# Householder tridiagonalisation of a 512 x 512 graph matrix: a new order inside each column, and interleaved matmul units placed twice per column

## The chip, the cores and the metric

One core of a Trainium2 chip runs the whole program in one launch. The metric is the time on the device in microseconds; the median of 3 runs of the kernel before is 5769.74 us (5765.54 to 5769.83).

## What is computed

Inputs are features x (16 batches, 512 nodes, 128 features) and a 512 x 512 adjacency matrix. Two layers follow each other, all in float32.

The first layer is a graph diffusion by eight explicit Euler steps:

```python
h = jnp.einsum('bnd,ed->bne', x, fc_in_w) + fc_in_b
def euler_step(h, _):
    ax = jnp.einsum('nm,bmd->bnd', adj_mx, h)
    f = alph * 0.5 * (ax - h) + h @ w_eff - h + x0
    return (h + dt * f, None)
```

and then a layer norm of x + h. The second layer needs the eigenvectors of the normalised Laplacian of the same adjacency matrix:

```python
L_norm = d_inv_sqrt[:, None] * (jnp.diag(deg) - A) * d_inv_sqrt[None, :]
_, U = jnp.linalg.eigh(L_norm)
agg = jnp.einsum('mn,bnd->bmd', U.T, features)
out = jax.nn.relu(agg @ W1 + b1) @ W2 + b2
return jnp.einsum('nm,bmd->bnd', U, out)
```

followed by a residual and a second layer norm. The eigendecomposition needs nothing from the first layer, and the second layer's other products need it.

## The kernel before

**Phases.** The matrix is first reduced to tridiagonal form by 511 Householder columns, one after the other. Then come the layer norm, a QL iteration on 32 leaves, five merge levels and the back transformation, and the second layer's products. The change touches the first phase alone. It is 3.3 of the 5.8 milliseconds.

**One column.** The matrix lies as T = 4 row tiles of 128 partitions. Column k works on `n_on = 4 - (k+1)//128` tiles: four tiles for k up to 126, three for 127 to 254, two for 255 to 382 (these are the "wide" columns), one for 383 to 510 (the "narrow" ones). Updates of the matrix are kept as pending pairs (u, r), up to some twenty of them. Every 16 columns the pending pairs become a panel, and `panel_stage` adds it to the matrix over the next 3 + n_on columns. Each column has its extra panel matmul in the tensor block (L700 to L724) and its extra addition in `householder` (L1343).

The order is written out by hand, in one program per engine, with semaphores between them:

- VectorE, `householder` (L1317): `x_ready(k)` says that the column x is written (L1425 of the column before). Then `next_reflected(k-1)` (L1290) takes the pivot column from the matrix (L1286 to L1300), forms z (L1309), and multiplies it with u (L1311). Then it takes one product of matrix and x per tile (L1352), HK (L1357), the fixing of the pending pair (L1364, L1368), the norm RN (L1371), the corrections (L1286, L1288), Q and RB (L1378, L1379), y (L1386), RQ (L1391), the sums CY (L1394, L1395), INVB and NINVB (L1398, L1399), beta (L1401 or L1406), BETAQ (L1404), TMP (L1418) and at last the next column (L1425).
- TensorE: it spreads x over all partitions by one transpose per tile (L681), sums z times u over the partitions (L653, or L656 for a narrow column, in `reflected_product`), computes the dots of x with the pending pairs (L688, one matmul per tile), then does its share of Euler units and the panel matmul, and after that the sum of CY (L729 or L733) and the pivot row of the pending pairs (L673).
- ScalarE copies x into the u column (L1109, L1110) and writes a unit vector beside it (L1113), takes root and norms out of the dots (L1115, L1117), scales ucN, MB, yq and tcol (L1129 to L1138), finishes u (L1146), and stores the results of the Euler units.
- GpSimd computes the signs SG, GZ, GT, HAL and P0 (L948 to L953) and U1 (L956, L957). In its spare time, one piece per column, it prepares the terms of the Euler polynomial (`preparations`, L919).

A narrow column does much of the same on one tile, and its product of matrix and x runs on TensorE (L695).

**Euler units.** The first layer is written as a polynomial in the adjacency matrix, and it runs on TensorE between the column's own matmuls. The generator `euler()` (L521) yields after every small portion of one product, a "unit". There are 551 of them. `euler_units(k)` says how many units a column takes, and all of them come after the dots:

```python
return 2 if 84 <= k < P + 84 else 1 if 8 <= k < 3 * P - 1 else 0
```

Units that are not used up in the columns run after the last one, `for _ in state: pass` (L735). The ScalarE program takes the same number of units per column, at the end of its column, after L1146, and stores each finished product with `euler_stored`. A product waits until the bank that it writes is stored, and the first product of a stage waits until all before it are. The products that use the polynomial's terms wait for `terms_ready`.

Of the kernel before, what the change touches and what calls it, by code (L numbers as in the profile page):

```python
# [112 lines left out]
def eig_gnn(nc, x, adj, alpha, w, d, fcw, fcb, W1, b1, W2, b2, consts, out, stop=99):  # L113
    ctx = ExitStack()
    with ctx:
# [40 lines left out]
        sparks = sb("sparks", [P, P])  # L156
# [64 lines left out]
        e_ready = sem("e_ready")  # L221
# [163 lines left out]
        MB, SPART = small[:, 32:33], small[:, 33:34]  # L385
# [37 lines left out]
        def euler_units(k):  # L423

            return 2 if 84 <= k < P + 84 else 1 if 8 <= k < 3 * P - 1 else 0
# [68 lines left out]
        def _(pe):  # L494
# [26 lines left out]
            def euler():  # L521
# [82 lines left out]
                pe.wait_ge(terms_ready, 1)  # L604
                for grp in range(4):
                    cols = slice(grp * N, (grp + 1) * N)
                    for i in range(4):
# [9 lines left out]
                        for mat in (Mt, M2t):  # L617
# [8 lines left out]
                            yield  # L626
                    for third in (2, 1, 0):
# [20 lines left out]
            def reflected_product(k):  # L648

                tp, n_on, pp = window_of(k)  # L650
                pe.wait_ge(z_ready, k + 1)
                if n_on >= 2:
                    nc.tensor.matmul(ps[1][:, 0:1], ones[:, :], SPART, start=True, stop=True).then_inc(s_ready, 1)  # L653
                else:
                    pe.wait_ge(u_ready, k + 1)
# [4 lines left out]
            adds_done = 0  # L660
            for k in range(N - 1):
# [17 lines left out]
                if n_on > 1:  # L679
# [10 lines left out]
                last.then_inc(dots_ready, 1)  # L690
                if n_on == 1:
# [6 lines left out]
                for _ in range(euler_units(k)):  # L698
                    next(state, None)
# [205 lines left out]
        def _(pool):  # L905
            nc.gpsimd.memset(UR[:, :], 0.0).then_inc(pairs_zeroed, 1)
            z = Chain(pool, pool_chain)
            ts, tt = nc.gpsimd.tensor_scalar, nc.gpsimd.tensor_tensor
# [8 lines left out]
            ts(sparks[:, :], ident[:, 0:P], SPARK, None, ALU.mult).then_inc(constants_ready, 1)  # L917

            def preparations():  # L919
# [13 lines left out]
                for _ in range(32):  # L933
                    yield
# [65 lines left out]
        def _(act):  # L1000
# [101 lines left out]
            for k in range(N - 1):  # L1102
# [45 lines left out]
                for _ in range(euler_units(k)):  # L1148
                    next(state, None)
# [1054 lines left out]
```

## Time and profile before

| | us |
|---|---|
| median of 3 runs | 5769.74 |
| profiled execution, its own time | 5766.69 |
| its span | 5764.9 |
| mean granted TensorE clock | 0.584 |
| busy PE / DVE / ACT / POOL | 2979.9 / 4277.6 / 1168.7 / 772.8 |

The span is the time from the first to the last instruction of the profiled execution. Its own time is 1.8 us longer, and 3.1 us under the median of the runs. PE is TensorE, PEld its weight loads, DVE is VectorE, ACT is ScalarE, POOL is GpSimd. L1425 is line 1425 of the kernel. Busy shares are means over phases with different limits, so they are read stage by stage. A granted clock of 0.50 is TensorE at 1.2 GHz and 1.00 is 2.4 GHz. The records of the clock begin at 390 us, and a stretch without any record is printed as 1.00.

### The profile page before, as it was taken

To read this page: it belongs to the slowest core of one execution; us is meant where nothing else is said; L and a number is where in the kernel's file an instruction comes from. 1 tells how busy PE (TensorE), PEld (TensorE's weight loads), DVE (VectorE), ACT (ScalarE), POOL (GpSimd) and SP (SyncE) were. 2 spreads that over 40 slices of the span, in tenths; PEclk is the share of its full clock that TensorE was granted. 3 is DMA by queue.
4 is the path that set the end of the run, shared out by engine and by line. 5 is a ranking of instruction groups with operands and counts; after the bars stand their busy time and mean duration, and the time that the engine had idled before them with its cause. 6 is when DMAs were issued, how large, how long until landed. Compare 5 with 4: busy or idle time off the path is not lost.

```text
span 5764.9 us, 62262 instructions
## 1 busy us (share of the span) xinstructions
PE 2979.9 (52%) x10552; PEld 2130.6 (37%) x10553; DVE 4277.6 (74%) x24278; ACT 1168.7 (20%) x5396; POOL 772.8 (13%) x3659
## 2 busy tenths in 40 slices
PE   6888888888888887877666610000000001010277
PEld 5656666556556555455555510000000000000243
DVE  7888777666667666666676678888788898889624
ACT  2333333333333333333222200000000000000000
POOL 2122211111111121222112111111100000000000
PEclk9985556656655555555555555555555555555688
DMA  1000000000000000000000000000000000000000
GB/s 40 1 1 1 1 1 1 1 1 1 1 1 1 1 1 1 1 1 1 1 1 1 1 25 0 0 0 0 0 0 0 0 0 0 0 0 0 0 0 29
DMA packets 16075, 17.01 MB, mean 3 GB/s; under 512 B 3056, under 2 KB 12400, under 8 KB 15472
## 3 DMA queue, kind: packets, MB, share of 16 engines
q1 hardware_dynamic: 15216, 13.47, 0.7%
q14 instruction: 264, 2.16, 0.1%
q8 instruction: 83, 1.36, 0.1%
q10 hardware_dynamic: 512, 0.02, 0.0%
HBM read 9.25 MB, written 4.19 MB: 2 GB/s over the span
## 4 chain that ended last, share of the span: by engine, by line
DVE 51%; PE 28%; ACT 7%; issue 7%; POOL 5%; DVEq 1%; ACTq 0%; DMA 0%; POOLq 0%; another core or an unknown queue 0%
PE ps L688 9%; DVE h L2020 5%; PE ps L653 3%; PE ps L632 2%; PE ps L620 2%; DVE am L1286 2%; DVE c L1288 2%; DVE UR L1425 2%; DVE UR L1309 2%; DVE notafter L1300 2%; PE ps L640 1%; ACT c L1134 1%; PE ps L722 1%; POOL small L948 1%; DVE hT L1647 1%
## 5 line engine op out<-in xcount | busy, mean ns | idle before, releaser
L688 PE MATMUL ps<-UR 128*128 128x41 f32 (+17 forms) x2552 | 606.5, 382 | 0.6 <-issue 0.6
L688 PEld LDWEIGHTS ps<-UR 128*128 128x128 f32 x2552 | 569.9, 315 | 0.9 <-DVE UR L1425 0.8
L805 PE MATMUL ps<-ident,m 128*128 128x128 f32 x36 | 9.0, 428 | 822.6 <-DVE small L2120 822.6
L749 PE MATMUL ps<-ones,qs 32*1 32x1 f32 x16 | 1.5, 158 | 821.2 <-DVE qs L1755 821.2
L681 PE MATMUL ps<-ident,UR 128*128 128x128 f32 x1148 | 318.4, 409 | 188.3 <-DVE UR L1425 183.3
L948 POOL TENSOR_SCALAR small<-small 128x1 f32<-128x1 f32 x511 | 117.3, 229 | 2201.9 <-ACT small L1117 2184.4
L729 PEld LDWEIGHTS ps<-small,ones 128*128 128x128 f32 x766 | 190.3, 301 | 393.7 <-DVE am L1395 308.6
L1418 DVE SCALAR_TENSOR_TENSOR small<-small,ps 128x1 f32<-128x1 f32 x510 | 112.1, 220 | 295.8 <-PE ps L729 279.0
L673 PE MATMUL ps<-UR,ident 128*128 128x18 f32 (+2 forms) x1020 | 299.4, 381 | 46.7 <-DVE UR L1368 46.7
L1115 ACT ACTIVATE small<-ps 128x1 f32<-128x1 f32 x511 | 87.6, 171 | 1163.5 <-PE ps L688 1163.5
L805 PEld LDWEIGHTS ps<-ident,m 128*128 128x128 f32 x36 | 7.0, 223 | 824.6 <-DVE small L2120 824.6
L749 PEld LDWEIGHTS ps<-ones,qs 32*1 32x1 f32 x16 | 0.7, 75 | 822.1 <-issue 822.1
L2020 DVE RECIPROCAL h<-h 128x512 f32<-128x512 f32 (+2 forms) x50 | 295.6, 5913 | 1.7
L653 PE MATMUL ps<-small,ones 128*128 128x1 f32 x766 | 213.3, 348 | 149.1 <-DVE am L1311 144.6
L653 PEld LDWEIGHTS ps<-small,ones 128*128 128x128 f32 x766 | 180.8, 294 | 290.7 <-DVE am L1311 290.7
L673 PEld LDWEIGHTS ps<-UR,ident 128*128 128x128 f32 x1020 | 260.9, 314 | 57.7 <-DVE UR L1368 57.7
L1359 DVE RECIPROCAL small<-small 128x1 f32<-128x1 f32 x511 | 83.2, 163 | 265.0 <-ACT small L1115 262.3
L681 PEld LDWEIGHTS ps<-ident,UR 128*128 128x128 f32 x1148 | 176.4, 198 | 235.2 <-DVE UR L1425 229.9
L729 PE MATMUL ps<-small,ones 128*128 128x2 f32 x766 | 204.1, 336 | 98.1 <-DVE am L1395 91.0
L1129 ACT ACTIVATE c<-UR,small 128x4 f32<-128x4 f32 (+2 forms) x383 | 114.2, 298 | 688.0 <-DVE small L1398 688.0
L640 PE MATMUL ps<-G,hT 128*128 128x128 f32 x1024 | 241.1, 401 | 5.2 <-ACT hT L1084 5.2
L640 PEld LDWEIGHTS ps<-G,hT 128*128 128x128 f32 x1024 | 214.0, 299 | 30.4 <-issue 22.5
(687 smaller groups left out, 9130.0 us busy)
## 6 DMA issues: line engine op xcount, KB each, us to landing
out<-xs SPq DMA_DIRECT2D x4, 1024.0 KB, 4.5
m<-in_adj SPq DMA_DIRECT2D x1, 1024.0 KB, 5.2
before<-c_before SPq DMA_DIRECT2D x1, 1024.0 KB, 6.9
notafter<-c_notafter SPq DMA_DIRECT2D x1, 1024.0 KB, 8.1
sib<-c_sib SPq DMA_DIRECT2D x1, 448.0 KB, 9.7
eye<-c_eye SPq DMA_DIRECT2D x1, 256.0 KB, 2.7
iota<-c_iota SPq DMA_DIRECT2D x1, 256.0 KB, 3.0
leafsel<-c_leaf SPq DMA_DIRECT2D x1, 256.0 KB, 3.2
```

The source lines that it names most:

```text
L620: last = nc.tensor.matmul(ps[6 + n % 2][:, :], xs[:, j, b * D:(b + 1) * D], mat[:, j, :], start=(j == 0), stop=(j == T - 1))
L632: nc.tensor.matmul(ps[6 + n % 2][:, :], M3t[:, j, tile(m)], h[:, j, cols] if third else middle[:, j, :], start=(j == 0), stop=False)
L640: last = nc.tensor.matmul(ps[6 + n % 2][:, tile(i)], Zt[r][i][:, tile(m)], terms[STEP3 * third + r], start=(third == 2 and r == 0), stop=( ...
L653: nc.tensor.matmul(ps[1][:, 0:1], ones[:, :], SPART, start=True, stop=True).then_inc(s_ready, 1)
L673: nc.tensor.matmul(ps[4][:, 0:2 * npend], over(one), flat[:, tp, 2 * first:2 * k], start=True, stop=True).then_inc(pivot_row_ready, 1)
L681: last = nc.tensor.transpose(ps[0][:, j * P:(j + 1) * P], over(x_of(j)), ident[:, 0:P])
L688: last = nc.tensor.matmul(ps[2][:, 0:2 * npend + 3], over(x_of(j)), flat[:, j, 2 * first:2 * k + 3], start=(j == tp), stop=(j == T - 1))
L729: nc.tensor.matmul(ps[3][:, 8:10], ones[:, :], CY, start=True, stop=True).then_inc(cy_ready, 1)
L948: z.post(ts(SG, AL, 0.0, 0.5, ALU.is_ge, ALU.subtract))
L1286: h_(tt(mine.rearrange("p (t l s) -> p t l s", t=n_on, s=2), pairs[:, tiles, first:first + npend, :], swapped.unsqueeze(1).broadcast_to([P ...
L1288: return h_.mark(nc.vector.tensor_reduce(out[:, 0:n_on], mine.rearrange("p (t l) -> p t l", t=n_on), AX.X, ALU.add))
L2020: g(nc.vector.reciprocal(Rm, Rm))
```

## The change

It does five things. (1) `euler_units(k)` returns a pair: so many units between the spreading of x and the dots, and so many after the dots. Columns 8 and 9 take three after the dots, columns 10 to 254 one and one, columns 255 to 382 two after the dots. (2) In wide columns the sum of z times u (`reflected_product`) moves behind the dots, and the dots wait for the z and u columns of the column before (`zq_ready`, `u_ready`). (3) GpSimd forms HAL first, then P0, then GT, each with its own signal. (4) VectorE computes RB and INVB before y, and takes over ucN of wide columns and MB and tcol of narrow ones. A narrow column writes x and u with one instruction. (5) The unit vectors beside the pairs are written once at the start and no longer in every column, and the wait for the Euler terms moves behind the first products that don't need them.

```diff
-            return 2 if 84 <= k < P + 84 else 1 if 8 <= k < 3 * P - 1 else 0
+            return (0, 0) if k < 8 or k >= 3 * P - 1 else (0, 3) if k < 10 else (1, 1) if window_of(k)[1] > 2 else (0, 2)
...
                 pe.wait_ge(x_loaded, 16 * T)
-                pe.wait_ge(terms_ready, 1)
...
+                    if grp == 0:
+                        pe.wait_ge(terms_ready, 1)
                     for third in (2, 1, 0):
...
                     last.then_inc(row_ready, 1)
-                    if k:
-                        reflected_product(k - 1)
-                pe.wait_ge(xm_ready, k + 1)
-                pe.wait_ge(e_ready, k + 1)
+                for _ in range(euler_units(k)[0]):
+                    next(state, None)
+                if k <= narrow_from:
+                    pe.wait_ge(xm_ready, k + 1)
+                if k:
+                    pe.wait_ge(u_ready, k)
+                    pe.wait_ge(zq_ready, k)
                 for j in range(tp, T):
                     last = nc.tensor.matmul(ps[2][:, 0:2 * npend + 3], over(x_of(j)), flat[:, j, 2 * first:2 * k + 3],
                                             start=(j == tp), stop=(j == T - 1))
                 last.then_inc(dots_ready, 1)
+                if n_on > 1 and k:
+                    reflected_product(k - 1)
...
-                for _ in range(euler_units(k)):
+                for _ in range(euler_units(k)[1]):
                     next(state, None)
...
+            z.sync()
+            for t in range(T):
+                units = nc.gpsimd.tensor_copy(pairs[:, t, t * P:(t + 1) * P, 0], ident[:, 0:P])
+            units.then_inc(pairs_zeroed, 1)
...
-                for _ in range(32):
+                for _ in range(12):
                     yield
...
-                z.post(ts(SG, AL, 0.0, 0.5, ALU.is_ge, ALU.subtract))
-                z.post(ts(GZ, XN, 0.0, 0.5, ALU.is_le, ALU.subtract))
-                ts(GT, XN, 0.0, None, ALU.is_gt)
-                z.sync()
-                tt(HAL, AL, SG, ALU.mult)
+                z(ts(SG, AL, 0.0, 0.5, ALU.is_ge, ALU.subtract))
+                tt(HAL, AL, SG, ALU.mult).then_inc(signs_ready, 1)
+                z(ts(GZ, XN, 0.0, 0.5, ALU.is_le, ALU.subtract))
                 tt(P0, GZ, SG, ALU.mult).then_inc(signs_ready, 1)
+                ts(GT, XN, 0.0, None, ALU.is_gt).then_inc(signs_ready, 1)
...
-                if not final:
-                    nt, _, npp = window_of(k + 1)
-                    nc.scalar.activation(flat[:, nt, 2 * k + 4:2 * k + 5], ident[:, npp:npp + 1], ACT.Copy).then_inc(e_ready, 1)
...
-                    act.wait_ge(invb_ready, k + 1)
                     if n_on > 1:
-                        act.wait_ge(xm_ready, k + 1)
-                        nc.scalar.activation(ucN[:, 0:n_on], column_of(k, slice(tp, T), 0), ACT.Copy, scale=RQ)
-                    nc.scalar.activation(MB, below, ACT.Copy, scale=INVB).then_inc(mb_ready, 1)
-                    act.wait_ge(mb_ready, k + 1)
-                    act.wait_ge(y_done, k + 1)
-                    if n_on > 1:
-                        nc.scalar.activation(yq[:, 0:n_on], y[:, 0:n_on], ACT.Copy, scale=RQ)
...
+                        act.wait_ge(invb_ready, k + 1)
+                        nc.scalar.activation(MB, below, ACT.Copy, scale=INVB).then_inc(mb_ready, 1)
+                        act.wait_ge(y_done, k + 1)
+                        if after:
                             nc.scalar.activation(tcol[:, 1:n_on], y[:, 1:n_on], ACT.Copy, scale=INVB)
+                            act.wait_ge(mb_ready, k + 1)
+                            nc.scalar.activation(tcol[:, 0:1], y[:, 0:1], ACT.Identity, scale=MB,
+                                                 bias=sparks[:, after, 1:2]).then_inc(t_ready, 1)
...
+                        act.wait_ge(rq_ready, k + 1)
+                        nc.scalar.activation(yq[:, 0:n_on], y[:, 0:n_on], ACT.Copy, scale=RQ).then_inc(yq_ready, 1)
...
-                if not wide_now:
+                if k == narrow_from:
                     tt(u_now, x_now, below, ALU.mult).then_inc(xm_ready, 1)
...
-                dve.wait_ge(signs_ready, k + 1)
                 h_.wait(has_rn)
+                has_rb = h_.mark(nc.vector.reciprocal(RB, RN))
+                dve.wait_ge(signs_ready, 3 * k + 1)
                 has_q = h_.mark(stt(out=Q, in0=RN, scalar=HAL, in1=N2, op0=ALU.mult, op1=ALU.add))
-                has_rb = h_.mark(nc.vector.reciprocal(RB, RN))
+                if wide_now:
+                    dve.wait_ge(signs_ready, 3 * k + 2)
+                    h_.wait(has_rb)
+                    stt(out=INVB, in0=P0, scalar=8.0, in1=RB, op0=ALU.mult, op1=ALU.mult).then_inc(invb_ready, 1)
...
+                    h_.wait(has_q)
+                    nc.vector.reciprocal(RQ, Q).then_inc(rq_ready, 1)
+                    h_.post(stt(out=NINVB, in0=P0, scalar=-8.0, in1=RB, op0=ALU.mult, op1=ALU.mult))
+                    dve.wait_ge(xm_ready, k + 1)
+                    dve.wait_ge(rq_ready, k + 1)
+                    h_.post(ts(ucN[:, here], u_now, RQ, None, ALU.mult))
                     ts(beta, RN, P0, 2.0, ALU.mult, ALU.mult).then_inc(beta_ready, 1)
                     dve.wait_ge(beta_ready, k + 1)
-                    h_.wait(has_rq)
                     h_.post(tt(BETAQ, beta, RQ, ALU.mult))
                 else:
-                    h_(ts(beta, RN, P0, 2.0, ALU.mult, ALU.mult))
+                    h_.wait(has_q)
+                    has_rq = h_.mark(nc.vector.reciprocal(RQ, Q))
+                    dve.wait_ge(signs_ready, 3 * k + 2)
+                    h_.wait(has_rb)
+                    has_invb = h_.mark(stt(out=NINVB, in0=P0, scalar=-8.0, in1=RB, op0=ALU.mult, op1=ALU.mult))
+                    has_beta = h_.mark(ts(beta, RN, P0, 2.0, ALU.mult, ALU.mult))
                     if not final:
-                        dve.wait_ge(xm_ready, k + 1)
-                        h_.post(ts(ucN[:, here], u_now, RQ, None, ALU.mult))
+                        masks = lower[:, pp:pp + 2][:, ::-1]
+                        h_.wait(has_rq)
+                        h_.post(stt(out=ucN[:, 0:2], in0=x_now[:, 0:1].broadcast_to([P, 2]), scalar=RQ, in1=masks,
+                                    op0=ALU.mult, op1=ALU.mult))
+                        h_.wait(has_invb)
+                        has_mb = h_.mark(ts(MBS, masks, NINVB, None, ALU.mult))
+                        h_.wait(has_beta)
+                        dve.wait_ge(signs_ready, 3 * k + 3)
                         stt(out=U1, in0=AL, scalar=beta, in1=GT, op0=ALU.subtract, op1=ALU.mult).then_inc(u1_ready, 1)
...
+                        dve.wait_ge(y_done, k + 1)
+                        h_.wait(has_mb)
+                        h_.post(stt(out=tcol[:, 0:2], in0=MBS, scalar=y[:, 0:1], in1=sparks[:, (k + 2) % P, :],
+                                    op0=ALU.mult, op1=ALU.subtract))
                     next_reflected(k)
...
                 if not wide_now:
-                    ts(x_now, z[:, here], RQ, None, ALU.mult).then_inc(z_ready, 1)
+                    ts(x_now, z[:, here], RQ, None, ALU.mult).then_inc(zq_ready, 1)
+                    h_.wait(has_tmp)
+                    stt(out=pairs[:, tp, k + 1, :], in0=ucN[:, 0:2], scalar=TMP, in1=tcol[:, 0:2],
+                        op0=ALU.mult, op1=ALU.subtract).then_inc(x_ready, 1)
+                    return
```

## Rows read from the trace of the kernel before

**Rows 1.** The page: the chain that ended last, by engine.
```profile
DVE 51%; PE 28%; ACT 7%; issue 7%; POOL 5%; DVEq 1%; ACTq 0%; DMA 0%; POOLq 0%; another core or an unknown queue 0%
```

**Rows 2.** Windows of L1425 (one per column): window, us, DVE busy (count), clock.
```profile
96.50:663.50 567.00, 21.13 (x74) 0.76 0.00 1
663.50:1006.10 342.60, 9.71 (x43) 0.60 0.00 1
1006.10:1622.50 616.40, 19.04 (x85) 0.64 0.00 1
1622.50:1915.20 292.70, 9.63 (x43) 0.50 0.00 1
1915.20:2720.00 804.80, 28.42 (x128) 0.50 0.00 1
2720.00:3289.90 569.90, 27.84 (x127) 0.50 0.00 1
```

**Rows 3.** Waits of DVE in 663 to 1622 us: total, times, longest.
```profile
DVE small L1418 <- PE ps L729: 168.1, 117, 5.6
```

**Rows 4.** Timeline of two-tile column 297: start us, us, engine, line [idle before].
```profile
2180.04 0.22 DVE L1425 SCALAR_TENSOR_TENSOR UR<-c,small 128x2 f32<-128x2 f32 x1 [0.51 <-ACT c L1138]
...
2180.94 0.22 DVE L1309 SCALAR_TENSOR_TENSOR UR<-notafter,small,c 128x2 f32<-128x2 f32 x1
...
2181.60 0.59 PE L653 MATMUL ps<-small,ones 128*128 128x1 f32 x2 [0.59 <-DVE am L1311]
...
2182.05 1.02 PE L688 MATMUL ps<-UR 128*128 128x21 f32 x4
...
2182.90 2.06 PE L632 MATMUL ps<-hT,m 128*128 128x512 f32 x2
...
2183.40 0.23 DVE L1364 SCALAR_TENSOR_TENSOR ps<-small 128x1 f32<-128x1 f32 x1
...
2184.36 0.22 DVE L1378 SCALAR_TENSOR_TENSOR small<-small 128x1 f32<-128x1 f32 x1
...
2185.04 0.59 PE L729 MATMUL ps<-small,ones 128*128 128x2 f32 x2
...
2185.66 0.22 DVE L1418 SCALAR_TENSOR_TENSOR small<-small,ps 128x1 f32<-128x1 f32 x1 [0.22 <-PE ps L729]
...
2185.99 0.37 ACT L1138 ACTIVATE c<-c,sparks,small 128x1 f32<-128x1 f32 x1
...
2186.40 0.22 DVE L1425 SCALAR_TENSOR_TENSOR UR<-c,small 128x2 f32<-128x2 f32 x1 [0.51 <-ACT c L1138]
```

**Rows 5.** Timeline of narrow column 441.
```profile
2980.54 0.22 DVE L1425 SCALAR_TENSOR_TENSOR UR<-c,small 128x1 f32<-128x1 f32 x1
...
2981.06 0.59 PE L688 MATMUL ps<-UR 128*128 128x21 f32 x2
...
2982.02 0.23 POOL L948 TENSOR_SCALAR small<-small 128x1 f32<-128x1 f32 x1 [3.55 <-ACT small L1117]
...
2982.72 0.18 POOL L953 TENSOR_TENSOR small<-small 128x1 f32<-128x1 f32 x1
...
2983.35 0.15 DVE L1399 SCALAR_TENSOR_TENSOR small<-small 128x1 f32<-128x1 f32 x1
...
2984.97 0.22 DVE L1425 SCALAR_TENSOR_TENSOR UR<-c,small 128x1 f32<-128x1 f32 x1
```

**Rows 6.** Timeline of a four-tile column near 400 us, clock 0.50.
```profile
400.59 0.63 DVE L1352 SCALAR_TENSOR_TENSOR junk<-A,ps 128x461 f32<-128x461 f32 x1
...
407.95 1.11 PE L681 MATMUL ps<-ident,UR 128*128 128x128 f32 x4 [0.17 <-DVE UR L1425]
```

**Rows 7.** Chain of waits in the flush of units, clock 1.00: start, us, what.
```profile
3300.19 3.44 PE ps L632 x8
3303.62 2.69 PE ps L640 x24
```

**Rows 8.** Timeline of the end of the flush.
```profile
3335.12 1.14 PE L741 MATMUL ps<-junk,ones 128*128 128x127 f32 x8
...
3336.29 0.69 DVE L1449 COPY drow<-ps 128x512 f32<-128x512 f32 x1 [39.11 <-PE ps L741]
```

More of the change, by code:

```diff
@@ L155, in eig_gnn @@
         cI = sb("cI", [P, P])
-        sparks = sb("sparks", [P, P])
+        sparks = sb("sparks", [P, P, 2])
         swap = sb("swap", [2 * PANEL, 2 * PANEL])
@@ L384, in eig_gnn @@
         corr, y, z, ucN, tcol, y0, acorr, yq = (c4[:, i, :] for i in range(8))
-        MB, SPART = small[:, 32:33], small[:, 33:34]
+        MB, SPART, MBS = small[:, 32:33], small[:, 33:34], small[:, 34:36]
         scratch = [junk[:, :], eye[:, :, :].rearrange("p a b -> p (a b)"), leafsel[:, :], iota[:, :]]
@@ L660, in _ @@
             adds_done = 0
+            narrow_from = next(k for k in range(N) if window_of(k)[1] == 1)
             for k in range(N - 1):
@@ L1135, in _ @@
-                    if after:
-                        if n_on > 1:
-                            nc.scalar.activation(tcol[:, 1:n_on], y[:, 1:n_on], ACT.Copy, scale=INVB)
-                        nc.scalar.activation(tcol[:, 0:1], y[:, 0:1], ACT.Identity, scale=MB,
-                                             bias=sparks[:, after:after + 1]).then_inc(t_ready, 1)
-                    else:
-                        if n_on > 2:
-                            nc.scalar.activation(tcol[:, 2:n_on], y[:, 2:n_on], ACT.Copy, scale=INVB)
-                        nc.scalar.activation(tcol[:, 1:2], y[:, 1:2], ACT.Identity, scale=INVB,
-                                             bias=sparks[:, 0:1]).then_inc(t_ready, 1)
+                        act.wait_ge(invb_ready, k + 1)
@@ new lines, in _ @@
+                        nc.scalar.activation(MB, below, ACT.Copy, scale=INVB).then_inc(mb_ready, 1)
+                        act.wait_ge(y_done, k + 1)
+                        if after:
+                            nc.scalar.activation(tcol[:, 1:n_on], y[:, 1:n_on], ACT.Copy, scale=INVB)
+                            act.wait_ge(mb_ready, k + 1)
+                            nc.scalar.activation(tcol[:, 0:1], y[:, 0:1], ACT.Identity, scale=MB,
+                                                 bias=sparks[:, after, 1:2]).then_inc(t_ready, 1)
+                        else:
+                            if n_on > 2:
+                                nc.scalar.activation(tcol[:, 2:n_on], y[:, 2:n_on], ACT.Copy, scale=INVB)
+                            nc.scalar.activation(tcol[:, 1:2], y[:, 1:2], ACT.Identity, scale=INVB,
+                                                 bias=sparks[:, 0, 1:2]).then_inc(t_ready, 1)
@@ L1147, in _ @@
                                          bias=pairs[:, tp, k, 0:1]).then_inc(u_ready, 1)
-                for _ in range(euler_units(k)):
+                for _ in range(sum(euler_units(k))):
                     next(state, None)
@@ L1307, in next_reflected @@
                 else:
-                    dve.wait_ge(t_ready, k + 1)
-                    h_(stt(out=column_of(k, on, 1), in0=a1, scalar=BETAQ, in1=yq[:, here], op0=ALU.mult, op1=ALU.subtract))
+                    dve.wait_ge(yq_ready, k + 1)
+                    stt(out=column_of(k, on, 1), in0=a1, scalar=BETAQ, in1=yq[:, here],
+                        op0=ALU.mult, op1=ALU.subtract).then_inc(zq_ready, 1)
+                    dve.wait_ge(zq_ready, k + 1)
                     dve.wait_ge(u_ready, k + 1)
@@ L1389, in householder @@
                         nc.vector.tensor_copy(y[:, here], source).then_inc(y_done, 1)
-                h_.wait(has_q)
-                has_rq = h_.mark(nc.vector.reciprocal(RQ, Q))
                 if wide_now:
@@ L1396, in householder @@
                         op0=ALU.mult, op1=ALU.mult, accum_out=CY[:, 0:1]).then_inc(y_ready, 1)
-                h_.wait(has_rb)
-                stt(out=INVB, in0=P0, scalar=8.0, in1=RB, op0=ALU.mult, op1=ALU.mult).then_inc(invb_ready, 1)
-                h_.post(stt(out=NINVB, in0=P0, scalar=-8.0, in1=RB, op0=ALU.mult, op1=ALU.mult))
-                if wide_now:
+                    h_.wait(has_q)
+                    nc.vector.reciprocal(RQ, Q).then_inc(rq_ready, 1)
+                    h_.post(stt(out=NINVB, in0=P0, scalar=-8.0, in1=RB, op0=ALU.mult, op1=ALU.mult))
```

23 lines of the change are left out of this document (13 added, 10 removed).

## The prediction

> **What bounds the kernel now.** I read the page first: the chain that ended last is VectorE for half and TensorE for a quarter of the span, so neither engine alone is the limit [rows 1]. The next view is the windows by stage. L1425 writes one column, so its count in a window is the number of columns, and us by count is the price of one [rows 2]: 7.66 us (four tiles, one unit), 7.97 (four, two units), 7.25 (three, two), 6.81 (three, one), 6.29 (two, one) and 4.49 (narrow, none). The clock beside them is 0.50 wherever a column has one unit or none, and 0.60 and 0.64 where it has two: there a fifth to a quarter of the time runs at 2.4 GHz, the rest at 1.2. (The first window's 0.76 is no reading: its records start at 390 us, and the transposes run alike before that.) In the stage with two units TMP waits for the sum of CY, behind the units on TensorE: 168.1 us over 117 waits, 1.4 us each [rows 3]. A column of two tiles is not held by its unit: the dots start 2.01 us after x, the next x waits for ScalarE's tcol, 0.51 us [rows 4]. The narrow column is one chain of small steps [rows 5]. After the last column VectorE stands idle for 39.11 us until the 48 units left over are done [rows 8].
>
> **The cost of a unit.** A 512-wide unit takes 0.86 us of TensorE at 2.4 GHz (3.44 by four), one of three 128-wide products 0.67 (24 matmul records in 2.69, six each) [rows 7]. At 1.2 GHz they take 1.71 and 1.3 (2.06 with its tail for the wide one [rows 4]). A single step (one transpose, or half of one dots matmul) is 0.21 to 0.28 (1.02 for four [rows 4], 1.11 for four [rows 6]), 0.21 between starts.
>
> **The change, part by part.**
>
> *Nothing left to flush.* Counting the yields in order, all 551 units are placed: 6 in columns 8 and 9, 490 in columns 10 to 254, 55 in columns 255 to 282. What stays of the 39.11 us is the diagonal's ten matmul steps at 1.2 GHz and their latency, 2.6 us. **-36.5 us.**
>
> *Narrow columns, 127.* The dots can't start earlier than now, since the sum of z and u still stands before them (four-tenths of a microsecond of steps): 0.03 us at most. The gain is behind GpSimd. Now SG starts 1.48 us after x, P0 ends at 2.36, and NINVB starts at 2.81 [rows 5], as Q, RB, y, RQ and INVB stand between. In the new order HAL comes after SG, so Q, RB, y and RQ are done while P0 is made. P0 itself ends 0.05 later (one wait more in its chain), and NINVB starts with it at 2.42: 0.39 earlier. From NINVB to the next x it is 1.62 us now [rows 5]. ucN, MB, U1 and tcol replace beta's wait, ucN and U1; one wait on MB costs some 0.07 and the dropped wait for ScalarE gives back as much. Per column -0.38, 127 of them: **-48 us.** Bounds: 0.15 (if each new wait costs 0.07) to 0.45.
>
> *Two-tile columns without a unit, 283 to 382, 100 of them.* From column 297 [rows 4]: z is written 1.12 us after x (L1309), so the dots start at 1.2 in place of 2.01. The sum of z and u comes behind them, four steps later at 2.0, and takes 0.59: HK starts at 2.64, and L1364 0.33 later at 2.97, where it is at 3.36 now. Q no longer waits for P0 (now at 4.32): the corrections take 0.62, RB, Q, INVB and y 0.75, the sums of CY another 0.25, so L729 starts at 4.6 in place of 5.00. Behind it VectorE now has RQ, NINVB, ucN, beta and BETAQ, up to 5.25, and TMP starts at 5.31 in place of 5.62. tcol needs INVB, now 0.8 us earlier, and ScalarE no longer makes ucN first: it is ready by 5.0, and the 0.51 us of waiting are gone. x comes at 5.64, I take 5.7 against 6.29 with the panels in: **-59 us.** Bounds 0.2 (HK late by the sum, nothing gained by INVB) and 0.7. In columns 255 to 282 two units follow the dots; at 1.2 GHz they end near 5.7, past the 4.6 at which CY is ready: 6.4 instead of 6.29, **+3 us.**
>
> *Four tiles, 10 to 126, 117 columns.* x is spread by 1.13 us (four steps from 0.28). The unit follows, mean 1.38 us at 1.2 GHz over the 117 that fall there (counted by kind, with the prices above), then the dots, S = 1.18 + unit after x. Eight steps of dots, the sum (0.59) and the latency give HK at S + 2.33, and from HK to the next x it takes 2.98 to 3.1 as in the two-tile column. So a column is 6.6 us plus the unit, 8.0. The second unit is hidden, since it ends near S + 3.9, and CY is ready at S + 4.4. The panel's matmul (1.7 us) then is not: over the 7 columns in 16 that have a stage +0.4 on the mean. 8.4 in all at 1.2 GHz. There is a floor by VectorE: four L1352 of 0.56 between starts [rows 6] bring HK to 3.85 at best (3.3 in the last columns), a column of 6.85 to 6.4. What the clock gives is the unknown. Between the spreading and the second unit TensorE now has no wait left, up to 6 us of unbroken work where the kernel before had a gap at the sum of z and u. Stages with two units have the clock raised for a fifth to a quarter of the time [rows 2]. A stretch t at 2.4 GHz saves up to t where TensorE is the chain, which here is 5 of 8 us (spreading 0.85, unit 1.4, dots 1.7, the two sums 0.6 each): 0.25 x 8 x 5/8 = 1.3 us, and nothing where VectorE's floor takes over. Between 0 and 1.3 I take 0.6, nearest to the stages of rows 2 that have two units and gained half of it. 7.8 against a mean of 7.77 now: **0 us.**
>
> A rule of the Trainium skill bears on it ("TensorE: Matmul & The Clock Gate", Part 1): the throttled state is the default and activity releases it. By it the unbroken work would keep the clock up, which is the far end of rival (a) below. The trace agrees in part: the clock is raised in the stages with two units and in none with one, but for a quarter of the time [rows 2].
>
> *Three tiles, 127 to 254, 128 columns.* The same with three tiles: 5.92 plus a unit of 1.45, 7.37, +0.25 for panels, -0.4 for the clock: 7.22 against 7.10 now (85 at 7.25, 43 at 6.81): **+15 us.**
>
> *Units that must wait.* First products of a stage need everything stored. 17 of them fall on the place after the dots, behind a unit of the same column which ScalarE stores only at the column's end. The CY sum is queued behind them on TensorE. Some 0.8 us each: **+13 us.** Columns 0 to 9: -2. POOL's start-up copies lie in its idle time before column 0, and the terms are ready by column 57 while the first product that needs them comes in column 62: nothing.
>
> Sum: -36.5 - 48 - 59 + 3 + 0 + 15 + 13 - 2 = -114.5. The profiled execution took 5766.69 us, so 5652; the median is 3 us above it, so 5655.
>
> **The rivals.**
>
> (a) *The clock stays up.* More unbroken TensorE work raises it for half of the time and not a quarter, and the wide columns give twice the credit (1.2 and 0.8 us): 5655 - 70 - 51 = 5534. For it: rows 2, where the clock rises only in stages with two units. Against: a column at 2.4 GHz has half the busy time and lets it fall again. At the far end, with the clock up throughout, every column stands at VectorE's floor and its panels (6.95 us for four tiles, 6.1 for three, where three L1352 end 0.8 earlier): 5655 - 99 - 143 = 5413; of the 0.18 below I give that end 0.02.
>
> (b) *The reorder is eaten by its waits.* The sum of z and u, now last on TensorE, holds HK, and VectorE carries five more instructions: two-tile columns gain 0.2 and narrow ones 0.15: 5655 + 38 + 29 = 5722. For it: only 0.33 us of the 0.8 by which the dots move up get through in my own walk. Against: the 0.51 us of waiting for tcol is a measured idle time [rows 4].
>
> (c) *Slower: the unit before the dots stands on the chain at 1.2 GHz.* The credit of the clock is nil, so columns 10 to 254 pay the full 1.4 us ahead of the dots (+70 +51), and the dependent units cost double (+13): 5789. The point from which it decides is a gain of less than 0.1 us by the clock per wide column. For it: the clock is 0.50 in every stage with one unit. Against: 0.60 and 0.64 with two.
>
> (d) *The change doesn't do what it says*: units still remain at the end, since TensorE waits for terms or stores; some 30 us of the flush stay: 5685, inside the forecast.
>
> **How the numbers follow.** The forecast 5655 with (d) has 0.65 (own range 5600 to 5705), (a) and what lies towards it 0.18, (b) 0.12, (c) 0.05. Leaving out (c) and the farther half of (a), the range is 5550 to 5725. A measurement of this kernel can tell about 0.2%, 11.5 us, from no change. All but (c) are faster by more than that; of the ground between (b) and (c) I give 0.02 to "same". Faster 0.93, same 0.02, slower 0.05.
>
> **What would show it.** VectorE's idle time before L1449's counterpart near 2.6 us, no TensorE work between the last column and the diagonal. Narrow columns at 4.1 us, the last hundred two-tile columns at 5.7, without a wait for tcol. Four-tile columns near 7.8 and three-tile ones near 7.2, alternating between about 8 and 6.5, with a granted clock of 0.60 to 0.70. The forecast is wrong if the wide stages move by more than 0.4 us per column either way (the clock term), or if HK in a two-tile column does not start near 2.6 us.

## The result, and the profile after

The kernel after takes 5805.66 us (median of 5 runs, 5797.73 to 5813.46) where the kernel before takes 5769.74 (5 runs, 5755.87 to 5776.03): ratio 1.0066 [1.0049, 1.0083]. It is 0.7% slower, clear of the noise. The forecast was 5655 us, range 5550 to 5725. The profiled execution took 5805.66 us, its span is 5803.8, its mean granted clock 0.546. (The 0.584 of the kernel before holds 390 us without records, printed as 1.00. From 391 us on the two kernels have 0.55 before and 0.54 after.)

The first view is again the chain that ended last. ScalarE and GpSimd have all but left it (2% and 1%, where they had 7% and 5%, [rows 1]). VectorE and TensorE have taken their shares, 6 and 4 points more than before.

```profile
DVE 57%; PE 32%; issue 6%; ACT 2%; POOL 1%; DVEq 1%; ACTq 0%; DMA 0%; POOLq 0%; another core or an unknown queue 0%
```

The second view answers to [rows 2]: windows by stage, here of L1369, which runs once in each column. Columns: window, us, VectorE busy in that line (count), clock.

```profile
97.52:720.57 623.05, 11.29 (x74) 0.55 0.00 1
720.57:1067.17 346.60, 6.56 (x43) 0.59 0.00 1
1067.17:1718.96 651.79, 12.98 (x85) 0.53 0.00 1
1718.96:2044.71 325.75, 6.56 (x43) 0.53 0.00 1
2044.71:2228.54 183.83, 4.28 (x28) 0.63 0.00 1
2228.54:2810.21 581.67, 15.31 (x100) 0.50 0.00 1
2810.21:3366.05 555.84, 20.75 (x127) 0.50 0.00 1
```

Set beside the windows of before (the 804.80 us of [rows 2] cut at column 283), the sums are, in us:

| columns | before | after | change | forecast |
|---|---|---|---|---|
| 10 to 126, four tiles | 909.6 | 969.7 | +60.1 | 0 |
| 127 to 254, three tiles | 909.1 | 977.5 | +68.4 | +15 |
| dependent units, all within 10 to 254 | | in the two above | | +13 |
| 255 to 282 | 176.6 | 183.8 | +7.2 | +3 |
| 283 to 382, two tiles | 628.2 | 581.7 | -46.5 | -59 |
| 383 to 509, narrow | 569.9 | 555.8 | -14.1 | -48 |
| last x to the diagonal | 46.4 | 9.5 | -36.9 | -36.5 |

The changes add to 38, and 1 us more in the columns before 10 makes it the 38.9 by which the spans differ. So the last three rows gained 97.5 us where the forecast had 143.5, and columns 10 to 254 took 128.5 where the forecast had 28: a miss of 100 there and of 46 behind it. The clock of those stages is the second thing to see: 0.53 in columns 127 to 211, where the kernel before had 0.64 with the same number of units [rows 2].

The flush is gone. The timeline after the last column answers to [rows 8]: 2.59 us of idle time, and the forecast had 2.6.

```profile
3373.52 2.06 PE L752 MATMUL ps<-junk,ones 128*128 128x127 f32 x8
3375.61 0.69 DVE L1480 COPY drow<-ps 128x512 f32<-128x512 f32 x1 [2.59 <-PE ps L752]
```

**A two-tile column** (330) answers to [rows 4]. L1456 writes the column, L657 is the sum of z and u, L1367 is HK, L740 the sum of CY, L1445 TMP.

```profile
2502.34 0.22 DVE L1456 SCALAR_TENSOR_TENSOR UR<-c,small 128x2 f32<-128x2 f32 x1
...
2503.61 1.02 PE L697 MATMUL ps<-UR 128*128 128x23 f32 x4 [0.30 <-DVE UR L1317]
...
2504.46 0.57 PE L657 MATMUL ps<-small,ones 128*128 128x1 f32 x2
...
2505.06 0.22 DVE L1367 TENSOR_SCALAR small<-ps,small 128x1 f32<-128x1 f32 x1 [0.87 <-PE ps L657]
...
2506.95 0.59 PE L740 MATMUL ps<-small,ones 128*128 128x2 f32 x2 [1.93 <-DVE am L1407]
...
2507.73 0.22 DVE L1445 SCALAR_TENSOR_TENSOR small<-small,ps 128x1 f32<-128x1 f32 x1
...
2508.07 0.22 DVE L1456 SCALAR_TENSOR_TENSOR UR<-c,small 128x2 f32<-128x2 f32 x1
```

Measured from x: dots 1.27, HK 2.72, CY 4.61, TMP 5.39, next x 5.73. The walk ahead of the result had 1.2, 2.64, 4.6, 5.31 and 5.64.

**A narrow column** (442) answers to [rows 5]. L964 is SG, L967 P0, L1423 NINVB, L1428 ucN, L1431 MB, L1434 U1, L1437 tcol, L1290 the first correction of the next column.

```profile
3069.64 0.21 DVE L1449 SCALAR_TENSOR_TENSOR UR<-c,small 128x2 f32<-128x2 f32 x1
...
3071.18 0.23 POOL L964 TENSOR_SCALAR small<-small 128x1 f32<-128x1 f32 x1 [3.31 <-ACT small L1128]
...
3071.96 0.19 POOL L967 TENSOR_TENSOR small<-small 128x1 f32<-128x1 f32 x1
...
3072.18 0.16 DVE L1423 SCALAR_TENSOR_TENSOR small<-small 128x1 f32<-128x1 f32 x1
...
3072.38 0.21 DVE L1428 SCALAR_TENSOR_TENSOR c<-UR,small,lower 128x2 f32<-128x2 f32 x1
...
3072.51 0.22 DVE L1431 TENSOR_SCALAR small<-lower,small 128x2 f32<-128x2 f32 x1
...
3072.64 0.21 DVE L1434 SCALAR_TENSOR_TENSOR small<-small,erow 128x1 f32<-128x1 f32 x1
...
3072.84 0.22 DVE L1437 SCALAR_TENSOR_TENSOR c<-small,c,sparks 128x2 f32<-128x2 f32 x1
...
3072.98 0.17 DVE L1290 SCALAR_TENSOR_TENSOR am<-UR,ps 128x20 f32<-128x20 f32 x1
...
3073.97 0.22 DVE L1449 SCALAR_TENSOR_TENSOR UR<-c,small 128x2 f32<-128x2 f32 x1
```

NINVB starts 2.54 us after x (2.81 before, 2.42 forecast), but from NINVB to the next x it is 1.79 and not 1.62. The starts of L1428, L1431 and L1434 are 0.13 apart: each added instruction takes its place in VectorE's queue, though nothing waits for its result there.

**A long column.** Twelve columns stand out with 9.3 to 13.0 us (62, 70, 86, 122, 130, 146, 182, 190, 206, 242, 250 and 266), some 45 us in all more than the medians of their neighbours, 3.8 each. (Some early and panel columns take 9.4 to 10.3 us too, beside neighbours that are nearly as long.) The timeline of column 182, with x at 1487.12:

```profile
1488.09 1.92 PE L622 MATMUL ps<-m,xs 128*128 128x512 f32 x2
...
1491.55 0.22 DVE L1367 TENSOR_SCALAR small<-ps,small 128x1 f32<-128x1 f32 x1 [1.40 <-PE ps L657]
...
1494.57 0.39 ACT L1154 ACTIVATE UR<-ident,UR,small 128x1 f32<-128x1 f32 x1 [0.53 <-POOL small L973]
...
1494.86 0.57 ACT L1100 ACTIVATE hT<-ps 128x512 f32<-128x512 f32 x1
...
1495.49 1.22 PE L644 MATMUL ps<-G,hT 128*128 128x128 f32 x4 [3.98 <-ACT hT L1100]
...
1496.93 0.43 PE L740 MATMUL ps<-small,ones 128*128 128x2 f32 x2
...
1497.39 0.22 DVE L1445 SCALAR_TENSOR_TENSOR small<-small,ps 128x1 f32<-128x1 f32 x1 [3.27 <-PE ps L740]
```

The unit before the dots ends a product at 1490.0. The unit after the dots needs it stored. ScalarE makes the store (L1100) last in its column, behind u (L1154), 4.9 us later. TensorE stands for 3.98 us, the sum of CY is queued behind the waiting unit, and VectorE waits 3.27 us for that.

### The profile page after: what moved, and what is told of

It reads as the page before. It is cut to its first block, busy times and chain, and to the rows that moved or that the text cites. A ratio compares the mean times of both kernels' runs of the same rounds, so it can differ in the third digit from the quotient of the medians.

```text
span 5803.8 us, 60985 instructions
## 1 busy us (share of the span) xinstructions
PE 2919.0 (50%) x10553; PEld 2179.9 (38%) x10553; DVE 4394.0 (76%) x24660; ACT 957.3 (16%) x4248; POOL 822.0 (14%) x3664
## 4 chain that ended last, share of the span: by engine, by line
DVE 57%; PE 32%; issue 6%; ACT 2%; POOL 1%; DVEq 1%; ACTq 0%; DMA 0%; POOLq 0%; another core or an unknown queue 0%
PE ps L697 8%; DVE h L2051 5%; PE ps L687 4%; PE ps L636 3%; PE ps L644 3%; PE ps L622 2%; PE ps L657 2%; DVE small L1445 2%; DVE c L1296 2%; DVE UR L1456 2%; DVE ps L1374 1%; DVE am L1294 1%; DVE hT L1678 1%; PE ps L661 1%; DVE c L1414 1%
## 5 line engine op out<-in xcount | busy, mean ns | idle before, releaser
L697 PEld LDWEIGHTS ps<-UR 128*128 128x128 f32 x2552 | 588.5, 317 | 232.5 <-issue 134.9
L697 PE MATMUL ps<-UR 128*128 128x41 f32 (+17 forms) x2552 | 577.9, 371 | 47.3 <-DVE UR L1317 46.7
L1367 DVE TENSOR_SCALAR small<-ps,small 128x1 f32<-128x1 f32 x510 | 111.1, 218 | 442.0 <-PE ps L657 364.3
L687 PE MATMUL ps<-ident,UR 128*128 128x128 f32 x1148 | 337.3, 431 | 144.0 <-DVE UR L1456 138.8
L964 POOL TENSOR_SCALAR small<-small 128x1 f32<-128x1 f32 x511 | 117.2, 229 | 1958.7 <-ACT small L1128 1942.3
L740 PEld LDWEIGHTS ps<-small,ones 128*128 128x128 f32 x766 | 185.6, 298 | 535.0 <-DVE am L1407 477.8
L740 PE MATMUL ps<-small,ones 128*128 128x2 f32 x766 | 207.9, 341 | 283.6 <-DVE am L1407 278.8
L679 PE MATMUL ps<-UR,ident 128*128 128x18 f32 (+2 forms) x1020 | 301.0, 383 | 46.4 <-DVE UR L1378 46.4
L1154 ACT ACTIVATE UR<-ident,UR,small 128x1 f32<-128x1 f32 x510 | 197.1, 386 | 442.3 <-DVE small L1434 231.3
L1445 DVE SCALAR_TENSOR_TENSOR small<-small,ps 128x1 f32<-128x1 f32 x510 | 112.0, 220 | 196.2 <-PE ps L740 149.4
L1139 ACT ACTIVATE small<-lower,small 128x1 f32<-128x1 f32 x383 | 112.8, 295 | 679.2 <-DVE small L1393 679.2
L657 PE MATMUL ps<-small,ones 128*128 128x1 f32 x766 | 205.7, 338 | 1.6 <-DVE am L1321 1.6
```

Of the source, the lines that this page charges most:

```text
L679: nc.tensor.matmul(ps[4][:, 0:2 * npend], over(one), flat[:, tp, 2 * first:2 * k], start=True, stop=True).then_inc(pivot_row_ready, 1)
L687: last = nc.tensor.transpose(ps[0][:, j * P:(j + 1) * P], over(x_of(j)), ident[:, 0:P])
L697: last = nc.tensor.matmul(ps[2][:, 0:2 * npend + 3], over(x_of(j)), flat[:, j, 2 * first:2 * k + 3], start=(j == tp), stop=(j == T - 1))
L740: nc.tensor.matmul(ps[3][:, 8:10], ones[:, :], CY, start=True, stop=True).then_inc(cy_ready, 1)
L964: z(ts(SG, AL, 0.0, 0.5, ALU.is_ge, ALU.subtract))
L1154: nc.scalar.activation(pairs[:, tp, k, 0:1], ident[:, pp:pp + 1], ACT.Identity, scale=U1, bias=pairs[:, tp, k, 0:1]).then_inc(u_ready, 1)
```

## The experiments

Theory A: the loss of the wide stages is the stores that come late. Theory B: it is the clock, which gives less credit for a pair of units split around the dots than for two together. Theory C: the new order of the column itself costs time there. The recorded expectations use other letters: A is their theory D; B is C in runs 1 and 2 and A in run 6; C is R; their V is about the narrow column. Line numbers of the kernels that change only `euler_units` are those of the kernel after.

**1. The other parity of the placement.** One unit fewer in column 9 moves every later product by one place.

```diff
-... else (0, 3) if k < 10 else (1, 1) if window_of(k)[1] > 2 ...
+... else (0, 11 - k) if k < 10 else (1, 1) if window_of(k)[1] > 2 ...
```

> The changed kernel, but column 9 takes two units after the dots instead of three, so that every later unit changes its place (before the dots or after them). Theory D (a stage's first product that falls on the place after the dots waits for a store that ScalarE makes only at the column's end, 12 columns of 10.6 to 13 us where their neighbours take 7 to 8.5): those 12 long columns vanish, about 45 us less than the changed kernel, near 5760 us. Theory C (the loss is the unit before the dots and the clock, the long columns only show waits that come in another place): the long columns move elsewhere, 0 to 10 us.

5815.13 us, ratio to before 1.008 [1.0063, 1.0097]. The long columns from 62 on are gone, and others are there, eight of them between 17 and 42, at 10.4 to 15.7 us. Columns 10 to 83 pay 18 us more, columns 127 to 211 get 11 back:

```profile
97.37:738.70 641.33, 11.34 (x74) 0.54 0.00 1
1089.28:1729.71 640.43, 13.04 (x85) 0.52 0.00 1
```

The stall belongs to pairs of products and not to columns. Another parity moves it and doesn't cure it: the 45 us less that A's form in the expectation asked for did not come.

**2. Both units after the dots.**

```diff
-... else (1, 1) if window_of(k)[1] > 2 else (0, 2)
+... else (0, 2)
```

> The changed kernel with both units of columns 10 to 254 after the dots. Theory C (at 1.2 GHz the unit before the dots lies on the chain with its full 1.7 us, and two wide units one behind the other are what raises the clock): three-tile columns fall from 7.6 to about 7.0 us and the granted clock of that stage returns from 0.53 to 0.60 or more, together 100 us or more less than the changed kernel, near 5700. Theory R (the new order inside the column costs the wide columns, the place of the unit doesn't): within 20 us of the changed kernel. Theory D expects the long columns to stay, since the first unit of a stage still stands behind one of the same column.

5708.68 us, 0.9896 [0.988, 0.9913], which is 97 us under the kernel after. Windows of columns 10 to 83, 84 to 126, 127 to 211 and 212 to 254:

```profile
97.70:695.40 597.70, 11.35 (x74) 0.67 0.00 1
695.40:1028.57 333.17, 6.59 (x43) 0.62 0.00 1
1028.57:1638.19 609.62, 13.01 (x85) 0.61 0.00 1
1638.19:1942.21 304.02, 6.60 (x43) 0.59 0.00 1
```

The records of the clock begin at 179 us in this run, so the first row's 0.67 is too high; from 179 to 695.40 us it is 0.62. So the clock is back at 0.59 to 0.62. One edit undone gives a time under both kernels, so the loss is in the place of the unit, not in the order (against C).

The long columns stay, as expected. The same twelve take 9.3 to 12.3 us, and in sum only 10 us less than in the kernel after. So the stores that come late are hardly a part of these 97 us: they come with this number of units, whether the pair is split or not. Run 4 has them too.

**3. The new order with the units of before.** The same counts and places as before, and so with a flush at the end.

```diff
-... else (0, 3) if k < 10 else (1, 1) if window_of(k)[1] > 2 else (0, 2)
+return (0, 2 if 84 <= k < P + 84 else 1 if 8 <= k < 3 * P - 1 else 0)
...
-                for _ in range(12):
+                for _ in range(32):
```

> The changed kernel's order inside the columns with the units as before (one per column from 8, two from 84 to 211, all after the dots, 48 left to flush; GpSimd prepares the terms as late as before). If the order is a gain by itself and the placement of units the loss: narrow -14, two-tile columns about -55 over 128, wide ones 0.2 to 0.3 us each over 245, some -60, so near 5640 us with the flush of 39 us back. Theory R: no faster than 5770.

5658.15 us, 0.9808 [0.9792, 0.9824]. The order, with all other parts of the change that don't concern the units, is worth 111 us, in every stage: four tiles 882.6 (-27), three tiles 887.8 (-21), columns 255 to 382 756.2 (-49), narrow 556.0 (-14). Four of the windows:

```profile
96.59:642.36 545.77, 11.33 (x74) 0.50 0.00 1
979.22:1587.84 608.62, 13.04 (x85) 0.61 0.00 1
1587.84:1866.99 279.15, 6.60 (x43) 0.50 0.00 1
2623.24:3179.27 556.03, 20.82 (x127) 0.50 0.00 1
```

C has fallen. The median of this kernel is next to the forecast for the change, by an accident of other terms.

**4. The order of before with the new number of units**, two per column from 10 on, all after the dots, the terms' wait as in the kernel after.

```diff
-            return 2 if 84 <= k < P + 84 else 1 if 8 <= k < 3 * P - 1 else 0
+            return 0 if k < 8 or k >= 3 * P - 1 else 3 if k < 10 else 2
```

> The kernel before, its order inside the column unchanged, with two units in every column from 10 on as in the changed kernel (both after the dots), none left to flush, and the Euler terms prepared and waited for as in the changed kernel. Against the kernel before it shows what the number of units alone does: the flush of 37 us is saved and 117 columns more carry a second unit, at 0.3 to 0.5 us each plus the waits of the 12 dependent products: 5760 to 5800 us. If extra units were free there, 5735.

5800.92 us, 1.0062 [1.0045, 1.0079]. Columns 10 to 254 take 1879.0 us against 1818.7, so the number alone, with its long columns, costs 60 there and 10 in columns 255 to 282, and gives back the flush of 37. In the new order the same step (run 3 to run 2) costs 51 us net.

**5. The store ahead of the wait.** ScalarE stores the product of the unit before the dots at that place of its own program; the rest is the kernel after.

```diff
+                for _ in range(euler_units(k)[0]):
+                    next(state, None)
                 act.wait_ge(dots_ready, k + 1)
...
-                for _ in range(sum(euler_units(k))):
+                for _ in range(euler_units(k)[1]):
```

> The changed kernel, but ScalarE stores the unit that stands before the dots right there (ahead of its wait for the dots) and no longer at the end of its column. Theory D (a stage's first product behind a unit of its own column waits for a store made only at the column's end): the 12 columns of 9.3 to 13 us fall to their neighbours' 7 to 8.5 and none appear elsewhere, columns 11 to 19 shorten too, 45 to 60 us less than the changed kernel. The rival: what a long column costs is given back by its neighbours (moving the long columns with one unit less gained nothing in the sum), then under 15 us.

5753.06 us, 0.9973 [0.9963, 0.9984], 53 us under the kernel after. Eleven of the twelve long columns fall to 7.0 to 8.3 us. Column 266, whose units both stand after the dots, keeps its 9.3, and 148 is new with 10.0 (7.5 in the kernel after). Columns 10 to 254 take 1900.0 us in place of 1947.2. So the late stores cost the kernel after 47 to 53 us. The clock stays about where it was:

```profile
97.63:705.80 608.17, 11.32 (x74) 0.54 0.00 1
705.80:1045.81 340.01, 6.58 (x43) 0.60 0.00 1
1045.81:1677.07 631.26, 13.00 (x85) 0.53 0.00 1
1677.07:1997.66 320.59, 6.58 (x43) 0.51 0.00 1
```

This run also shows the walk's price at 1.2 GHz. From one x to the next, 88 of the 117 four-tile columns had a clock of 0.50 throughout; they took 8.30 us on the mean, and the walk had 8.4. Of the 128 three-tile columns 116 did, at 7.47 us, and the walk had 7.62. The others took 7.50 and 7.09 us. (Which products fall on them differs too, so not all of this gap need be the clock's.) So 41 of the 245 columns saw a raised clock. In the kernel after it was 51, and in run 2 it was 160. At 0.50 throughout, the columns of these two kernels are close to each other: 8.61 and 8.59 us with four tiles, 7.69 and 7.52 with three.

**6. Both units before the dots**, with the early store of run 5: `(2, 0)` in place of `(1, 1)`.

> As the kernel with the early store, but both units of columns 10 to 254 stand before the dots, one behind the other. Theory A (two wide units back to back are what raises the clock, a split pair is not): the granted clock of columns 127 to 211 rises from 0.53 to 0.60 or more although the order of the column is otherwise the same. By the chain alone, at 1.2 GHz, the second unit adds 1.5 us to each of 245 columns less what it hid behind VectorE, some 0.9 to 1.3 us each, so 200 to 300 us more than with one unit before the dots; the clock gives back up to half. If the clock stays at 0.53, theory A falls.

6000.9 us, 1.0409 [1.0392, 1.0427]. Columns 10 to 254 take 238 us more than in run 5: nearly 1 us per column for the second unit on the path. But the clock rises. These are windows of columns 127 to 211 of before, after and this run: window, us, TensorE busy (count), clock. The row of this run is printed for all engines, and TensorE is the first, ahead of its weight loads, VectorE, ScalarE and GpSimd:

```profile
1006.10:1622.50 616.40, 526.23 (x1951) 0.64 0.00 1
```

```profile
1067.17:1718.96 651.79, 580.54 (x1990) 0.53 0.00 1
```

```profile
1158.97:1874.23 715.26, 524.15 (x1990) 398.43 (x1989) 451.47 (x2821) 180.46 (x809) 115.34 (x596) 0.61 0.00 1
```

TensorE is busy for 85%, 89% and 73% of the stage, and the clock is 0.64, 0.53 and 0.61. (A busy share is in part made by the clock, since the same work lasts longer at 1.2 GHz. But 73% with a raised clock against 89% without one can't be that alone.) The clock goes with whether the two units stand together. B holds for this stage. With both units together behind the dots (runs 2 and 4) it is 0.61 too. It also holds for columns 10 to 83 (0.59 here, 0.54 in run 5) and 212 to 254 (0.61 and 0.51), but not for columns 84 to 126 (0.61 and 0.60).

**7. The narrow column filled better.** MB stands between the pivot column and z of the next column, where VectorE waits for its own result, and tcol behind it.

```diff
-                        h_.wait(has_invb)
-                        has_mb = h_.mark(ts(MBS, masks, NINVB, None, ALU.mult))
...
+                        next_reflected(k, lambda: h_.post(ts(MBS, masks, NINVB, None, ALU.mult)))
```

> The changed kernel, but in narrow columns VectorE computes MB between the pivot column and z, and tcol after z, where it waited. Theory V (a narrow column is a chain on VectorE in which each added small instruction costs its 0.13 us, so MB and tcol ate the gain of the new sign order): 0.2 us less per narrow column, 4.38 to about 4.15, 28 us less than the changed kernel. If the chain is held elsewhere (GpSimd's signs, the dots), no change in the narrow columns.

5782.38 us, 1.0025 [1.0014, 1.0035]. Columns 383 to 509 take 531.3 us in place of 555.8, 4.18 us each in place of 4.38. So two small instructions off the chain are worth 0.19 us.

```profile
2815.88:3347.17 531.29, 20.82 (x127) 0.50 0.00 1
```

**8. Where the sum of z and u stands.** Run 3 with `reflected_product` ahead of the dots again, as before.

> The kernel with the new order and the units as before (5658 us), but with the sum of z and u ahead of the dots again in wide columns. By the walk of the prediction the dots then start 0.8 us later, HK comes 0.4 us earlier and L1364's counterpart 0.3 to 0.4 us later, so a two-tile column goes from 5.8 to about 6.1 us (38 us over 128 columns); three- and four-tile columns with one unit, which VectorE's matrix products hold until 2.8 to 3.9 us, change by 0 to 0.2 us. In all 5690 to 5730. The rival: the place of the sum doesn't matter and the gain of the two-tile columns is all from INVB and tcol; then within 12 us of 5658.

5702.39 us, 0.9892 [0.9876, 0.9909], 44 us over run 3. By the profile, which was taken of an execution of 5710.91 us, a two-tile column takes 6.08 in place of 5.90 us, and a four-tile column with one unit 7.50 in place of 7.38. Moving the sum behind the dots is a gain, 0.06 (four tiles, two units) to 0.18 us a column, and 40% of what the order brings. The 128 two-tile columns have 23 us of it, where 38 were expected.

**9. The parts that pay, together.** Order of the change, narrow columns as in run 7, one unit in each column from 8 to 509 (in narrow columns behind the sum of CY), a second one in columns 163 to 211 alone, none left to flush, the Euler terms prepared as late as before.

```diff
+            return (0, 0 if k < 8 or k >= N - 2 else 2 if P + 84 - 49 <= k < P + 84 else 1)
...
+                    for _ in range(euler_units(k)[1]):
+                        next(state, None)
```

> The changed kernel's order with the narrow columns' VectorE order of the earlier run (MB before z, tcol after it), one unit in every column from 8 to 509 after the dots (in narrow columns after the sum of CY, where TensorE waits), a second one in 49 three-tile columns, none left to flush. Against the kernel with the units as before (5658): narrow order -24, flush -38, 79 second units fewer at 0.4 to 0.7 each, -30 to -50, narrow units 0 to +0.3 us each if a wide unit of 1.7 us doesn't fit: near 5570, between 5540 and 5610.

**5579.98 us, 0.9673 [0.9657, 0.9689]**: 226 us under the kernel after and 190 under before. Windows of columns 84 to 126, 127 to 211, and the narrow ones:

```profile
641.94:953.59 311.65, 6.58 (x43) 0.50 0.00 1
953.59:1537.73 584.14, 13.02 (x85) 0.57 0.00 1
2575.22:3140.65 565.43, 20.79 (x127) 0.51 0.00 1
```

A second unit less saves 25 us over 43 four-tile columns (0.59 each, against run 3) and 24.5 over 36 three-tile ones (0.68 each). A unit in a narrow column costs 0.27 (565.4 against 531.3 in run 7, over 127).

## Why the prediction was wrong

Two chains of single steps lead from before to after. By median: 5770 with the new number of units is 5801 (run 4), with the new order too 5709 (run 2), and with the pair split around the dots 5806. The number costs 31, the order gives 92. With the order first it is 5658 (run 3) and then 5709 (run 2): the order gives 112, the number costs 51. The last step is the same in both: the split costs 97 and decides the sign.

- **The step that failed is the first: the unit before the dots at no net cost.** The forecast took 0.6 and 0.4 us per wide column as the clock's credit, on the reasoning that TensorE, with no gap left, would be raised as much as in the stages with two units. (It worked out 1.3 and took half, for which it had no row. And 0.64 is 28% of the time at 2.4 GHz, a little more than its quarter.) With the stalls removed (run 5) a four-tile column takes 8.10 us and a three-tile one 7.44, against 8.4 and 7.62 in the walk at 1.2 GHz. Against that walk the credit was 0.3 and 0.18, together 58 us of the 121 that were forecast: 63 us short. Run 5 bears the walk out where the clock was 0.50 throughout (8.30 and 7.47 us). What was missing were columns with a raised clock, 41 of 245 there against 160 with the pair together (run 2). Part of the reading of [rows 2] was right: the clock is raised in the stages with two units. That it matters whether they stand together could not be seen there, since before had no stage with two units apart. The Trainium skill ("TensorE: Matmul & The Clock Gate", Part 1) has activity release the throttle. Here the busier TensorE had the lower clock: 92% and 0.53 in run 5 against 73% and 0.61 in run 6, which differ only in the place of one unit. So how busy TensorE is gave no forecast here, and the measurement decides.
- **Dependent units.** The mechanism was foreseen, and mis-sized: 17 times 0.8 us, 13 in all. Twelve stand out, at 3.8 each, and it was 47 in all by run 5. It explains a part of the miss against the walk, not the 97 us of the split, since run 2 has these waits too. The walk costed the store as one late step; in truth it comes behind u, which is ScalarE's last work in the column, so a stall lasts until the column is all but over (3.98 us in column 182).
- These two make 97 of the 100 us by which columns 10 to 254 missed. Those columns are 0.51 and 0.53 us slower than before (four and three tiles), past the 0.4 that the prediction had named as the sign of a wrong clock term.
- **Narrow columns.** -14 in place of -48. NINVB came forward by 0.27 and not 0.39, since SG starts 0.06 later (after x, 1.54 against 1.48) and P0 ends 0.97 after that in place of 0.88. And two more instructions between NINVB and the first correction, which the walk had at nothing, took 0.23 (0.80 in place of 0.57). Run 7 gives 0.19 of that back.
- **Two-tile columns.** Right in mechanism, and in column 330 within a tenth of a microsecond at each point of the walk; -46.5 and -59 differ by 0.13 us a column. The sum of z and u behind the dots was no trap (run 8).
- **The flush**: -36.9, forecast -36.5.
- **The rivals.** (c) came true in time (5789) and in mechanism: the unit stands on the chain and half of the clock's credit is missing (63 of 121 us). It had 0.05. Its own point of decision was too strict: a credit of half the forecast was enough once the stalls were there and the narrow gain was not. (a) did not come: TensorE was busier in columns 127 to 211 (89% against 85%), and the clock was raised less, not more. Its "against", that a column with less busy time lets the clock fall, is not borne out by run 6 (73% and 0.61). (b) is refuted for the two-tile columns by runs 3 and 8. Its narrow half came true: a gain of 0.11 us, under its 0.15, and for the reason that it gave, more instructions on VectorE. (d) did not happen, no unit is left.

The chances were the second error. The wide columns were a difference of two terms of over 100 us each, one of them (the clock) with no row of the same pattern, and yet a zero credit had 0.05.

What stays open: columns 84 to 126 have split pairs too and kept 0.59 to 0.60, as in the kernel before, but had 0.55 in run 1, where each product falls on the other place. So which products make the pair matters too, and no run here tells how. Nor was it separated by a run how much of the split's 97 us is the clock and how much the place, since putting a unit before the dots changes both. The small gap between the columns at 0.50 throughout (0.02 and 0.17 us, behind run 5) speaks for the clock as the larger part. That is a reading of the traces, not a test.

## What to carry to other kernels

Measure a bundle's parts one by one: here an order worth 111 us was hidden by a number and a placement of units that together cost 148. When work is interleaved into an in-order queue, look up where the *other* engine releases it. A store at the end of its program turns one dependent unit into a wait of half a column, and everything queued behind waits with it. Filler is cheapest where the engine is idle for another reason (0.27 us in a narrow column against some 0.6 for a second unit in a wide one), and each small instruction ahead of the chain costs its issue, 0.13 us here, even when its result is not needed yet.

## What was not expected of the hardware

The granted clock did not follow TensorE's busy share. In the same 85 columns, with two units in each, it was 0.61 to 0.64 with two units back to back, before or behind the dots (runs 2, 4 and 6, and before), and 0.53 with the same two units on either side of the dots. The first form had 85% (before), 88% (run 2) or 73% busy time (run 6), the second 89% (after) or 92% (run 5). (The products are the same in all of these but the kernel before, and four-tile columns 84 to 126 don't follow the pattern.) And a kernel can do without the raised clock: run 9, the fastest of all, has 0.50 to 0.51 in every stage but columns 127 to 211, where 49 columns have two units. It carries 79 second units fewer than run 3, so it is no measure of what the clock is worth.
